# Rotary step of an attention kernel: who multiplies q by the sines

## What is computed

```python
q = q * cos + _rotate_half(q) * sin          # _rotate_half(x) = concat([-x2, x1])
k = ...
scores = jnp.einsum('bhqd,bhkd->bhqk', q, k) * scale
scores = jnp.where(causal[None, None], scores, -1e9)
attn = jax.nn.softmax(scores, axis=-1)
out = jnp.einsum('bhqk,bhkd->bhqd', attn, v)
```

## Time and profile before

| | |
|---|---|
| runs | 2499.43, 2504.86, 2507.26 us (median 2504.86) |
| the profiled execution, its time | 2505.75 us |
| the profiled execution, its span | 2503.9 us |
| TensorE's granted clock, mean over the span | 0.984 |
| busy share: TensorE matmuls, VectorE, ScalarE, GpSimd | 95%, 59%, 45%, 38% |
| attention begins | 617 us |

### The profile page before, as it was taken

One profiled execution on the slowest core, in us unless ns is written; L12 is line 12 of the kernel. 1 busy time (PEld: TensorE's weight loads), 2 busy tenths in 40 slices (PEclk: granted clock), 3 DMA queues, 4 the chain that ended last, 5 costly groups with the idle time before them and its releaser, 6 DMA issues.

```text
span 2503.9 us, 38985 instructions
## 1 busy us (share of the span) xinstructions
PE 2379.1 (95%) x11840; PEld 1965.5 (78%) x11840; DVE 1482.6 (59%) x3641; ACT 1135.9 (45%) x2217; POOL 940.5 (38%) x815
## 2 busy tenths in 40 slices
PE   6999999996699999999999999999999999999998
PEld 5777877775588878887887888788888878888876
DVE  4343334433376667666676666566666666666765
ACT  3443525343244545444544445354544444454544
POOL 1000000000354545444454545354544545454543
PEclk9999999998799999999999999999999999999999
DMA  5676767577512131212212133413121221313110
GB/s 197 196 284 165 263 188 245 185 226 264 210 43 103 34 111 51 93 47 96 86 53 102 43 143 101 135 34 112 43 94 55 89 102 35 108 36 110 35 47 22
DMA packets 103727, 287.19 MB, mean 115 GB/s; under 512 B 9056, under 2 KB 42336, under 8 KB 92512
## 3 DMA queue, kind: packets, MB, share of 16 engines
q1 hardware_dynamic: 101408, 280.53, 33.2%
q10 hardware_dynamic: 2112, 4.19, 0.4%
HBM read 200.80 MB, written 83.89 MB: 114 GB/s over the span
## 4 chain that ended last, share of the span: by engine, by line
PE 61%; issue 7%; DVE 3%; ACT 3%; DMA 1%; POOL 0%; DVEq 0%; SPq 0%; POOLq 0%; ACTq 0%
PE qb L1060 14%; PE ob L1111 14%; PE scores L1075 13%; PE ob L1096 12%; PE ptb L1085 8%; DVE pT L1018 2%; ACT pT L984 2%; DMA xT<-xT_parts 1%; ACT prob L974 1%; POOL prob L948 0%; DVE nmax L1004 0%; DVE q_sin L1013 0%; DVE q_cos L1014 0%; DVE prob L1004 0%; DVE q_sin L1012 0%
## 5 line engine op out<-in xcount | busy, mean ns | idle before, releaser
L948 POOL TENSOR_TENSOR prob<-prob,rinv 128x896 f32<-128x896 f32 (+7 forms) x512 | 583.4, 1149 | 374.7 <-DVE rinv L1036 370.7
L984 ACT ACTIVATE pT<-ptb 128x512 fp32r<-128x512 f32 x576 | 334.9, 593 | 541.4 <-PE ptb L1085 534.5
L974 ACT ACTIVATE prob<-prob,nmax 128x896 f32<-128x896 f32 (+7 forms) x512 | 396.6, 775 | 358.5 <-DVE nmax L1004 351.3
L1096 PE MATMUL ob<-pT,v_sb 128*128 128x512 f32 x1728 | 509.5, 413 | 17.8 <-DVE pT L1018 15.4
L1075 PE MATMUL scores<-kT,qT 128*128 128x512 f32 (+3 forms) x2304 | 507.2, 350 | 19.9 <-issue 11.6
L1075 PEld LDWEIGHTS scores<-kT,qT 128*128 128x128 f32 x2304 | 386.3, 189 | 78.3 <-issue 19.9
L1018 DVE TENSOR_TENSOR pT<-ptb,pT 128x512 fp32r<-128x512 f32 x576 | 390.5, 687 | 95.2 <-ACT pT L984 84.3
L1004 DVE CUSTOM_DVE_ANT_0 prob<-scores,mask 128x896 f32<-128x896 f32 (+7 forms) x512 | 384.6, 753 | 61.8 <-issue 46.4
L1060 PE MATMUL qb<-xT,wq 128*128 128x512 f32 x1536 | 381.7, 399 | 35.6 <-DMA xT<-xT_parts 28.6
L1060 PEld LDWEIGHTS qb<-xT,wq 128*128 128x128 f32 x1536 | 296.0, 193 | 103.2 <-issue 27.7
L1096 PEld LDWEIGHTS ob<-pT,v_sb 128*128 128x128 f32 x1728 | 295.1, 190 | 89.1 <-DVE pT L1018 46.2
(11 more groups left out here) (71 smaller groups left out, 1943.5 us busy)
## 6 DMA issues: line engine op xcount, KB each, us to landing
wq<-w_parts SPq DMA_DIRECT2D x128, 512.0 KB, 3.8
w_parts<-stage SPq DMA_DIRECT2D x32, 1024.0 KB, 4.9
ff_raw<-in_ffw SPq DMA_DIRECT2D x56, 384.0 KB, 3.7
k_parts<-stage SPq DMA_DIRECT2D x128, 128.0 KB, 2.4
v_parts<-stage SPq DMA_DIRECT2D x64, 256.0 KB, 3.6
w_raw<-in_wqo SPq DMA_DIRECT2D x32, 512.0 KB, 5.7
kT<-k_parts SPq DMA_DIRECT2D x16, 1024.0 KB, 7.6
v_sb<-v_parts SPq DMA_DIRECT2D x16, 1024.0 KB, 8.4
```

Of the source, the lines that this page charges most:

```text
L948: nc.gpsimd.tensor_tensor(prob[:, n % 2, h, 0:W], prob[:, n % 2, h, 0:W], rinv[:, hd % 8:hd % 8 + 1].broadcast_to([P, W]), ALU.mult)\
L974: nc.scalar.activation(prob[:, n % 2, j, 0:W], prob[:, n % 2, j, 0:W], ACT.Exp, bias=nmax[:, hd % 8:hd % 8 + 1], scale=-1.0, accum_out=rsu ...
L984: nc.scalar.activation(pT[:, t % 3, HI], ptb[t % 2][:], ACT.Copy).then_inc(pT_hi, 1)
L1096: mm = nc.tensor.matmul(ob[:], v_sb[:, e % 2, x, j], pT[:, t % 3, y], start=(j == 0 and (x, y) == (HI, HI)), stop=(is_last(kind, n, j) and ...
```

## The change

The swapped halves of q leave PSUM as two plain copies of 64 x 512 on ScalarE. VectorE, which now waits for these copies, makes only the product with the cosines. GpSimd multiplies the swapped copy by the sines in SBUF, waits on its own semaphore, and then makes the sum as before. Two semaphores are new (`q_swapped`, `q_scaled`). The sine table changes its sign layout because it is now applied after the swap. The planner is told the new chain with new costs.

```diff
     if kind == "Q":
-        return [("dve", "Q", n, j, 1.97, 0.05), ("pool", "Q", n, j, 1.1, 0.1),
+        return [("act", "Q", n, j, 1.1, 0.1), ("dve", "Q", n, j, 0.61, 0.1), ("pool", "Q", n, j, 2.2, 0.1),
                 ("act", "QL", n, j, 0.55, 0.1), ("pool", "QL", n, j, 1.1, 0.1)]
...
+            pool.wait_ge(tab2, 16)
...
                     elif kind == "Q":
                         pool.wait_ge(q_read, it1 * UNITS + n + 1)
+                        x = n // AHEAD % 2 * CHUNK
+                        nc.gpsimd.tensor_tensor(q_sin[:], q_sin[:], qtab[:, 1, x:x + CHUNK], ALU.mult)\
+                            .then_inc(q_scaled, 1)
+                        pool.wait_ge(q_scaled, it1 * UNITS + n + 1)
                         nc.gpsimd.tensor_tensor(q_cos[:], q_cos[:], q_sin[:], ALU.add).then_inc(q_turned, 1)
...
+                    elif kind == "Q":
+                        act.wait_ge(q_done, it1 * UNITS + n + 1)
+                        act.wait_ge(q_split, it1 * UNITS + n)
+                        nc.scalar.activation(q_sin[0:HALF], qb[HALF:P], ACT.Copy)
+                        nc.scalar.activation(q_sin[HALF:P], qb[0:HALF], ACT.Copy).then_inc(q_swapped, 1)
...
                     elif kind == "Q":
                         x = n // AHEAD % 2 * CHUNK
-                        cos, sin = (qtab[:, i, x:x + CHUNK] for i in range(2))
-                        dve.wait_ge(q_done, it1 * UNITS + n + 1)
-                        dve.wait_ge(q_split, it1 * UNITS + n)
-                        nc.vector.tensor_tensor(q_sin[0:HALF], qb[HALF:P], sin[HALF:P], ALU.mult)
-                        nc.vector.tensor_tensor(q_sin[HALF:P], qb[0:HALF], sin[0:HALF], ALU.mult)
-                        nc.vector.tensor_tensor(q_cos[:], qb[:], cos, ALU.mult).then_inc(q_read, 1)
+                        dve.wait_ge(q_swapped, it1 * UNITS + n + 1)
+                        nc.vector.tensor_tensor(q_cos[:], qb[:], qtab[:, 0, x:x + CHUNK], ALU.mult).then_inc(q_read, 1)
...
-        "qtab": np.stack([np.concatenate([cosT, cosT]), np.concatenate([sinT, -sinT])], 1),
+        "qtab": np.stack([np.concatenate([cosT, cosT]), np.concatenate([-sinT, sinT])], 1),
```

More of the change, by code:

```diff
@@ L795, in attention @@
         q_done = sem("q_done")
+        q_swapped = sem("q_swapped")
+        q_scaled = sem("q_scaled")
         q_read = sem("q_read")
@@ L813, in attention @@
         stored = sem("out_stored")
-        start_counts = [(q_done, UNITS), (q_read, UNITS), (q_turned, UNITS), (q_hi, UNITS), (q_split, UNITS),
+        start_counts = [(q_done, UNITS), (q_read, UNITS), (q_swapped, UNITS), (q_scaled, UNITS), (q_turned, UNITS), (q_hi, UNITS), (q_split, UNITS),
                         (s_done, HPB), (max_ready, HPB), (exp_done, HPB),
```

## The result

The changed kernel takes 2550.27 us in the median of four executions (2547.42 to 2562.48), the kernel before 2504.84; the ratio is 1.0194, with a 95% interval of 1.0157 to 1.0231. It is slower, by 45 us; the forecast was 2537, the range 2519 to 2557. The profiled execution took 2549.87 us, its span 2548.1 us: 44.2 more than before.

What follows compares the result with a forecast made beforehand. The prediction took TensorE, 99% busy in a group of eight, as the bound. 2505.75 + 33 for the late S(4,3) - 1 for small waits gave 2538 us profiled, so 2537 for the median; range 2519 to 2557.

Steps and rivals of the forecast that it cites:

- TensorE sets the end; the others can only make it wait: In the attention TensorE is busy 1703 of 1744 us; changes elsewhere only gain its waits or make it wait.
- VectorE's relief is worth nothing: About 177 us less VectorE work was valued at nothing; the rival that it wins, 2464 to 2485 us, had 0.07.
- the release of `qb`: Freeing the buffer for the next Q: 1.9 us after Q instead of 2.1, said not to matter.
- The chain Q(7) to S(4,3), six steps: In step 4, through ScalarE, VectorE and GpSimd: S(4,3) 2.05 us later at 16 places, 33 us in sum.
- The low end of the range: Cosine product first on VectorE, QL(7) before NORM(4,0) on GpSimd: 0.85 us late at 16 places, 14 us, 2519.
- T(4,0) holds: In step 4, T(4,0), moved by the same 2.05 us, comes at 1174.5, after NORM(4,3) ends at about 1173.6.
- Gain elsewhere, 1 us: Outside the chain to S(4,3), 1 us was taken as gain for TensorE's small waits.
- more places than S(4,3): Rival: new list order makes T(4,0) or T(5,0) wait too, 16 us per further 1 us; 2558 to 2590; chance 0.07.
- its upper end: A second NORM (1.25 us) ahead of QL(7) on GpSimd: 3.3 us late at 16 places, 53 us, 2557.
- The port: Rival: GpSimd and VectorE shut each other out, 128 x 1.3 = 166 us, 2671 us; chance 0.02.

Runs made afterwards that it cites:

- order_only: The kernel before, same instructions, with the lists the planner makes from the new costs (entries of ScalarE's copies taken out): 2560.59 us, ratio 1.0219.
- the three on the old lists: Changed kernel on lists planned with the old costs: alone, with GpSimd's product early, and also with S(n,3) later on TensorE: 2630.57, 2568.20, 2580.48 us.
- relief_only: The kernel before, VectorE's two products with the sines cut from 512 to 8 columns, nothing moved to another engine: 2497.64 us, ratio 0.9977.
- all_mended: Changed kernel with GpSimd's product and mask building no longer waiting early, and QL(7), T(2,1) and step 4's cosine product moved ahead in the lists: 2509.39 us.
- old_lists: Changed kernel's instructions with the lists planned for the kernel before, ScalarE's copies put right behind the last PV: 2630.57 us, ratio 1.0498.
- tab2_moved: Changed kernel with GpSimd's wait for the sine table moved from before building identity and mask to before its first work on q: 2549.13 us.
- short_product: Changed kernel with GpSimd's added product cut from 512 to 8 columns: 2532.94 us, ratio 1.0099.
- early_product: Changed kernel with GpSimd's product waiting only for the swapped copies, not for VectorE's cosine product: 2534.43 us, ratio 1.0099.
- both_t_first: Changed kernel with T(2,1) ahead of QL(6) in ScalarE's list and ahead of S(3,3) in VectorE's: 2544.73 us, ratio 1.0158.

## Why the prediction was right, and where it was off

- *TensorE sets the end; the others can only make it wait.* Right in the main: in the sixth group TensorE's work is 112.2 to 112.5 us in every run whose granted clock is 1.00 there, and the time follows its waits. In the four runs with a clock of 0.99 there (order_only and the three on the old lists) it is 114.2 to 115.2 us. So a wait can cost more than its length, which the prediction did not count.
- *VectorE's relief is worth nothing.* Right in the groups (relief_only, 113.06 us, and all_mended). At the start it was worth 6 to 7 us, through the waits of the first four Qs, their clock and the issue of an xT load, and that was no part of the sum. The prediction set aside the release of `qb` because the next Q comes 9 us later at the least; of the first four Qs that is wrong, they stand 6.8 to 7.8 us apart and each waits for it. In the changed kernel the gain did not show: its waits ahead of them are 2.2 to 2.5 us, as before.
- *The chain Q(7) to S(4,3), six steps.* Right in order and cause. The prediction had QL(7) end 7.82 us after the copies begin (1168.88 less 1161.06); it was 1298.16 + 1.28 less 1291.85, so 7.59. Half of the difference is VectorE's, whose cosine product began 1.73 us after the copies and not 1.84; the rest is a few hundredths at each of GpSimd's steps. S(4,3) was late by 1.81 us instead of 2.05; in this group 0.08 us was in hand after all (0.20 us between QL(7) and S(4,3) before, 0.12 after). Copies 0.59 us each (0.60 taken), product 1.293 us (1.30), GpSimd's wait on itself 1295.71 less 1295.63 = 0.08 (0.08). The term came to 29 us instead of 33. The low end of the range, 0.85 us with both lists the other way round, was met too: 0.88 in old_lists.
- *T(4,0) holds.* Right: no new wait of T for NORM in the changed kernel (4.9 us against 5.1).
- *Gain elsewhere, 1 us.* This is the step that was off: there was no gain but a second place, PV(2,1) in step 3, with 11 us. The prediction came near it in a rival (more places than S(4,3), with ScalarE's copies ahead of T's) but looked for it only at T(4,0) and T(5,0), and gave it 0.07. The new lists put T(2,1) behind S(3,3) on VectorE, which the planner's rule gives when it is played through step 3, as was done only for step 4. That 2550 us lies in the range all the same is in part luck: the range was drawn for S(4,3) alone, and its upper end stands for a second NORM ahead of QL(7), which did not happen.
- *The wait for the sine table.* It is in the change and has no term in the sum. It cost 4.8 us at the first Q (tab2_moved). In the profiled execution this does not show in the total up to the fifth Q, 0.6 us, because the first stage ended 2.2 us earlier there and the five Qs and what stands between them took 2.0 us less.
- *The port.* No sign of it: L1022 and GpSimd's sum keep their times in the changed kernel (next section), and short_product, which takes GpSimd's load back, leaves 28 us standing. The Trainium skill, page "SBUF — State Buffer", section "Who interferes with whom", states that a VectorE instruction with at most one SBUF input, outside the modes that use two ports, does not contend with GpSimd; L1022 has one, and its 684 to 692 ns in all 128 cases agree.

That the sum of both places, 30 in all 16 steps 4 (29, and 1.6 in one where the granted clock was 0.54 behind the wait) and 11, with 3 us of small change made 44 is shown in the trace; that each is caused by what is said here is shown by mending each alone (early_product, short_product, both_t_first) and all at once. Open is why the clock falls behind some waits and not behind others of the same length.

## What to carry to other kernels

When one engine is full and the rest are half idle, moving work between the idle ones is not free: look up each semaphore that the full engine meets with no time in hand, and count the new latency there, hand-off by hand-off. When the order of the in-order queues comes from a planner, a change of its costs is a second change; run the old instructions with the new lists and the new with the old, as either can cost more than the edit. And before one list is mended, ask whether another engine's list holds up the same step, since then the first mend shows nothing. Last, count a wait of TensorE of some microseconds as more than its length, since the clock can fall behind it, and read such a mend at a distance within one step rather than in the whole time.

## What the runs showed of the hardware

```profile
L987 ACT ACTIVATE q_sin<-qb x128: 593/595/598, 625.7 to 2466.7; 64x512 f32<-64x512 f32 x128
L988 ACT ACTIVATE q_sin<-qb x128: 588/589/592, 626.3 to 2467.4; 64x512 f32<-64x512 f32 x128
L957 POOL TENSOR_TENSOR q_sin<-q_sin,qtab x128: 1267/1293/1302, 627.8 to 2469.2; 128x512 f32<-128x512 f32 x128
L960 POOL TENSOR_TENSOR q_cos<-q_cos,q_sin x128: 1262/1287/1298, 629.1 to 2470.6; 128x512 f32<-128x512 f32 x128
L1022 DVE TENSOR_TENSOR q_cos<-qb,qtab x128: 684/687/692, 627.0 to 2468.5; 128x512 f32<-128x512 f32 x128
```

ScalarE's copy of 64 partitions takes as long as one of 128 (0.59 us against 0.59 to 0.60), as VectorE's product does, so an exchange of halves costs two full instructions on either engine. The two copies do not overlap: the second starts 0.61 us after the first (1291.85 and 1292.46). GpSimd's product takes 0.204 us for 8 columns and 1.293 us for 512; from these two, an estimate is 0.19 us and 2.16 ns for each column.

TensorE's granted clock falls to its lower level (0.50) for a microsecond or more behind some waits. Behind the 3.04 us of T(4,0) in old_lists it did in 13 of 16 groups, and the 12 matmuls of W(3) and what follows took 1.5 us more. Behind the 1.8 us of S(4,3) in the changed kernel it did in one of 16 (0.54 from 827 to 829 us), and that step is 3.4 us longer instead of 1.8. Behind waits of 2.3 to 2.5 us ahead of the first Qs the clock was 0.63 in the kernel before, and behind 1.4 to 1.6 us it was 1.00 in relief_only; but the changed kernel's fourth Q, behind 2.5 us, had 1.00 too. So the length of the wait alone does not settle it in these traces.
